# TensorE's expert program as a loop over pairs of experts instead of groups of four

## The reference, cut to what matters

```python
x = x + _L0_gnn_ref(_layernorm(x), adj, ...)         # attention with adj as bias, then a feed-forward net
x = x + _L0_ffn_ref(_layernorm(x), ...)
# in _L0_ffn_ref, with E1 = 8 outer and E2 = 4 inner experts, DIM = 384, HID = 1024:
slots2 = einsum('bGksd,bGksem->bGkemd', yn, disp2)    # 256 rows for each of the 32 experts (k, e)
u = einsum('bGkemd,kedh->bGkemh', slots2, w1) + b1
v, gate = split(u, 2, axis=-1)
act = v * gelu(gate)
o = einsum('bGkemh,kehd->bGkemd', act, w2) + b2
out2 = einsum('bGkpd,bGksp->bGksd', o, comb2)
out = einsum('bGPd,bGgP->bGgd', out2, comb1)
```

## Time and profile before

| | us |
|---|---|
| median of 3 runs | 3081.5 (3080.99 to 3088.55) |
| the profiled execution, own time | 3075.87 |
| its span, first to last instruction | 3074.1 |
| span of the experts' stage on TensorE, first expert matmul to last | 2141.69 to 2999.57 |
| mean granted TensorE clock | 0.975 of full speed |

### The profile page before, as it was taken

How to read it: one execution, slowest core, us unless ns; L and a number is a source line. 1 busy time by engine, 2 the same in 40 slices (tenths; PEclk the granted TensorE clock), 3 DMA queues, 4 the chain that set the end, 5 groups by cost and what they waited for, 6 DMA issues and landing times. The chain is left out here.

```text
span 3074.1 us, 63137 instructions
## 1 busy us (share of the span) xinstructions
PE 2860.1 (93%) x21971; PEld 2754.7 (90%) x21971; DVE 1899.1 (62%) x3029; ACT 1510.8 (49%) x3986; POOL 1474.9 (48%) x1486
## 2 busy tenths in 40 slices
PE   2899999999999999999999848997999999999996
PEld 2899999999999999999999738997999999999993
DVE  3466666666666666666666425664776766676764
ACT  3355554545454555545554425675454444454540
POOL 0344444343534444443444324552776766676760
PEclk9899999999999999999999969998999999999999
DMA  3010101010100101010101034553666656665899
GB/s 130 13 42 26 46 26 46 26 46 25 42 28 31 41 26 46 26 46 26 46 26 41 20 94 119 150 148 119 200 209 199 209 182 198 193 208 173 252 322 340
DMA packets 276793, 321.59 MB, mean 105 GB/s; under 512 B 17304, under 2 KB 275608, under 8 KB 276504
## 3 DMA queue, kind: packets, MB, share of 16 engines
q1 hardware_dynamic: 267960, 307.17, 32.1%
q10 hardware_dynamic: 8704, 12.58, 1.1%
HBM read 260.97 MB, written 58.72 MB: 104 GB/s over the span
## 5 line engine op out<-in xcount | busy, mean ns | idle before, releaser
L1567 PE MATMUL u_bank<-x_in,x_w 128*128 128x256 f32 x4608 | 584.1, 286 | 28.5 <-issue 20.8
L1567 PEld LDWEIGHTS u_bank<-x_in,x_w 128*128 128x128 f32 x4608 | 576.9, 194 | 31.4 <-issue 31.4
L949 POOL TENSOR_TENSOR hT_lo<-h_tmp,hT_hi 128x512 fp32r<-128x512 f32 x192 | 246.6, 1285 | 454.3 <-DVE hT_hi L838 453.1
L1724 POOL TENSOR_TENSOR x_aT<-x_act,x_aT 128x512 fp32r<-128x512 f32 x128 | 299.3, 2339 | 216.7 <-ACT x_aT L1632 216.7
L411 PE MATMUL m_bank<-yT_hi,w_hi 128*128 128x256 f32 x1152 | 341.5, 296 | 1.5 <-ACT h_tmp L683 1.5
L1623 ACT ACTIVATE x_gelu<-u_bank,x_b1T 128x256 f32<-128x256 f32 x256 | 121.4, 474 | 444.9 <-PE u_bank L1567 444.9
L411 PE MATMUL m_bank<-yT_hi,w_lo 128*128 128x256 f32 x1152 | 323.4, 281 | 0.0
L411 PE MATMUL m_bank<-yT_lo,w_hi 128*128 128x256 f32 x1152 | 323.4, 281 | 0.0
L1720 POOL TENSOR_TENSOR x_w<-expert_raw,x_w 128x768 fp32r<-128x768 f32 x128 | 274.3, 2143 | 102.1 <-DVE x_w L1663 102.1
L683 ACT ACTIVATE h_tmp<-m_bank,b1c 128x256 f32<-128x256 f32 x384 | 156.9, 470 | 273.5 <-PE m_bank L411 273.1
L1579 PE MATMUL o_bank<-x_w,x_aT 128*128 128x384 f32 x1536 | 289.3, 336 | 1.8 <-POOL x_aT L1724 1.8
(11 more groups left out here) (216 smaller groups left out, 6939.2 us busy)
## 6 DMA issues: line engine op xcount, KB each, us to landing
expert_raw<-in_L_ffn_w_dram SPq DMA_DIRECT2D x384, 384.0 KB, 5.0
ws_raw<-in_L_ffn_w_slot_dram SPq DMA_DIRECT2D x32, 576.0 KB, 7.1
x_in<-in_x_dram SPq DMA_DIRECT2D x32, 384.0 KB, 3.4
x_res<-in_x_dram SPq DMA_DIRECT2D x32, 384.0 KB
residual<-f_sb SPq DMA_DIRECT2D x32, 384.0 KB, 2.5
yn<-yn_sb SPq DMA_DIRECT2D x32, 384.0 KB, 2.5
expert_out<-x_o SPq DMA_DIRECT2D x64, 192.0 KB, 3.2
slots2T<-residual SPq DMA_DIRECT2D x8, 1536.0 KB, 11.7
```

Source lines behind the costliest of these rows:

```text
L949: nc.gpsimd.tensor_tensor(hT[i % 3][1][:], h_tmp[i % 2][:], hT[i % 3][0][:].bitcast(F32), ALU.subtract).then_inc(hl.sem, 1)
L1567: mm = pe.matmul(u_bank[n % BANKS][:, g, :], w1s[i % 2][a][:, c, g, c2 * P:(c2 + 1) * P], xT[e % 2][b][:, c, :], start=c == 0 and j == 0, ...
L1724: nc.gpsimd.tensor_tensor(aTs[i % 2][1][:], aT[i % 2][:], aTs[i % 2][0][:].bitcast(F32), ALU.subtract).then_inc(al.sem, 1)
```

## The change

TensorE no longer uses over_experts. Its program writes out two experts, then has a loop over pairs, from 1 to 14, with two experts in its body, and then two experts again. So there are 14 trips and 13 taken branches. body loses the argument k, which it did not use, and the parity e takes the place of e from 0 to 3; down(x - 1, 1 - e, ...) names the other parity's bank. The calls for each expert, their order, the buffers and the waited values are the same as before. The other four engines keep their loops over groups of four.

```diff
-            def body(x, k, e):
+            def body(x, e):
                 up(x, e, 0)
                 if past(x, 1):
-                    down(x - 1, (e - 1) % E2, PIECES - 1)
+                    down(x - 1, 1 - e, PIECES - 1)
                 for i in range(1, PIECES):
                     up(x, e, i)
                     down(x, e, i - 1)
-            over_experts(pe, body)
-            down(NX - 1, E2 - 1, PIECES - 1)
+            for e in range(2):
+                body(e, e)
+            with pe.Fori(1, NX // 2 - 1) as pair:
+                for e in range(2):
+                    body(pair * 2 + e, e)
+            for e in range(2):
+                body(NX - 2 + e, e)
+            down(NX - 1, 1, PIECES - 1)
```

## The result

The median is 3043.7 us (3041.47 to 3048.47, 4 runs) against 3081.24 us (3076.13 to 3088.55, 4 runs) before: a ratio of 0.9878, with a 95% interval of 0.9855 to 0.9902. The profiled execution took 3044.84 us, its span is 3043.1 us.

The account below looks back on a forecast made before the run. TensorE was taken to bound the kernel, losing 34.3 us at five back edges of its experts' loop; all other terms were 0. 3075.87 - 34.3 = 3041.6 us, or 3047.2 from the median; forecast 3045 us, range 3037 to 3057.

Parts of the forecast that it names:

- the loss of 34.3 us: Experts' stage, 125 units between down groups: 833.45 us against 799.1 without stalls, lost at five taken back edges of TensorE's loop.
- a lower clock: 11.4 us of the 34.3 us, at four of five back edges, taken for a consequence of TensorE's 22.9 us of gaps.
- Why an edge stalls: At each taken back edge the trip's whole program is read again through q8; two gaps wait for the first pieces.
- expected some 40: Sign of being right: instruction queue q8 brings some 40 transfers instead of 95.
- The trip gets shorter: TensorE's experts' loop: a pair's 768 matmuls and loads, below the layer's 859, stay on the engine; -34.3 us.
- what could make it wrong: Room on the engine depends on more than length, such as where the loop begins among the blocks q8 brings.
- More back edges: TensorE's pair loop has 13 taken branches: taken as 0 us, bounded from above by 13 x 0.46 = 6 us.
- The other engines' cover: DVE, POOL, ACT and DMA have 30% to spare in an undisturbed trip, so they do not hold TensorE up: 0 us.
- two cases for how the runs differ: Median falls to 3041.6 us if runs differ by stall length, to 3047.2 us if by something else.
- The pair doesn't stay either: Rival: the pair's program is read again at 13 edges, 6.86 us each, 89 us in all, 3134 us; chance 0.06.
- no change: Rival: DVE, POOL or weights' transfers fall behind over 32 experts and take up the time, up to 3081 us; chance 0.03.
- the clock drops stay: Rival: only the gaps go and lower clock remains there or elsewhere; gain 22.9 us, 3056 us; chance 0.04.

Follow-up runs that it names:

- experiment 7: The change with 56 more already-met wait instructions (112 waits) at the end of each pair trip on TensorE: 3127.51 us, ratio to before 1.0144.
- experiment 8: The change with 36 more already-met wait instructions (72 waits) at the end of each pair trip on TensorE: 3070.51 us, ratio to before 0.9961.
- experiment 2: The kernel before with 64 more instructions (already-met waits) on TensorE ahead of the first expert, loop over groups of four kept: 3046.2 us, ratio 0.9893.
- experiment 3: The kernel before with 256 more instructions (already-met waits) in TensorE's set-up, a whole block: 3081.66 us, ratio 1.0004.
- experiment 4: The kernel before with 200 more instructions (400 already-met waits) in TensorE's set-up, single run: 3046.72 us, against 3083.74 us for the kernel before.
- experiment 9: The change with 32 more instructions (64 already-met waits) in TensorE's set-up, single run: 3042.3 us.
- experiment 5: The kernel before with six experts in TensorE's loop body, four ahead and four behind, 3 taken edges: 3062.72 us, ratio 0.9934.
- experiment 1: The change with four experts in TensorE's loop body instead of two, head and tail of two kept, 6 taken edges: 3071.66 us, ratio to before 0.9966.

## Why the prediction was right

*What bounds the kernel, and the loss of 34.3 us.* The stretch of 125 units fell from 833.45 to 799.16 us, 34.3 us less, as the sum had it (833.45 - 799.1). Both parts went, the 22.9 us of gaps and the 11.4 us that the prediction calls a lower clock. That the clock's fall follows from the gaps was inferred from five edges; experiments 7 and 8 show it with idle time of another origin. The size of the clock's part was too large. At the first edge, where the clock stayed 1.00, the window is 3.60 us too long and the gaps are 3.06, so 0.54 is neither; at that rate 2.7 us of the 11.4 are the rest that experiment 8 shows without a lower clock, and some 8.7 us are clock. The sum of both, and so the forecast, is not touched by it.

*Why an edge stalls.* The reading was that the trip's program is fetched again. q8 with 41 blocks instead of 95 fits it (expected some 40), and every kernel with gaps has its 9 blocks for each missed edge of a group of four, or 12 for one of six. Nine is one more than the eight blocks of the trip.

*The trip gets shorter, and so stays.* The step was right, by a comparison with the layer's loop. Its ground was coarser than the cause. The text read the limit as a length, between the layer's trip (909 instructions; its 859 matmuls and loads are 856 by the trace's branches, the window took in a few more) and the group's 1,611. Experiments 2 to 4 show that 1,611 stay as well if they lie in 7 blocks, and not if they lie in 8. The prediction named this as what could make it wrong; it could not do so for a pair, whose 807 lie in 4 or 5 blocks (experiment 9). Seven stay, and eight do so only when no further block is brought, which fits a store of eight blocks of which one is the block read ahead, past the loop's end. That size is an estimate from these runs: five blocks (experiment 9) and seven (2 and 4) stay, eight are read again at every taken edge of the kernel before and of experiment 3, and eleven in experiment 5. That one block of the eight is taken by reading ahead is my reading of where the limit lies. Experiment 1 fits it: the branch comes some 24 instructions into the eighth block, and at the one edge that didn't miss q8 had brought nothing; in the kernel before the branch comes some 40 into it, and its five edges all miss. One such edge was traced, so this detail is argued, not shown.

*More back edges, 0 us.* Right: 799.16 us with 13 taken edges and with none. The upper bound of 6 us did not count.

*The other engines' cover.* Right: no new wait in the stage.

*The base.* 3043.7 lies between the prediction's two cases for how the runs differ, 3041.6 and 3047.2 us, and the kernels without gaps spread over about 7 us themselves (3041.47 to 3048.47), so that some of the spread has other causes. Outside of the 125 units the profiled execution after took 3.3 us longer than that of before, in parts that the change leaves alone: the stage began 1.8 us later, and what follows the last but one down group took 2.0 us longer, less 0.6 at the first matmuls.

*The rivals.* "The pair doesn't stay either" (0.06) is out by the q8 row, "no change" (0.03) by the waits, "the clock drops stay" (0.04) by the clock of 1.00 over the stage.

## What to carry to other kernels

If an engine idles with the releaser "issue" at the same place of every trip of a loop, look at the instruction queue over that trip: transfers in each trip mean that the loop's program is read again. On TensorE here, loops in four to seven blocks of about 256 instructions (every matmul counts two, with its weight load) ran their back edges for nothing; a loop in eight blocks cost 6.9 us per edge and one in eleven 6.3, gaps and lower clock together. Halving a trip that just doesn't fit cost nothing at either of the two places tried, and unrolling it entirely gained nothing over that.

## What was not expected of the hardware

Where a loop lies in the program can be worth 1.1% of a kernel without a change to the loop: 64 idle instructions ahead of it took 3079.89 to 3046.2 us. And one program at the limit (experiment 1) missed at five of its six edges in the execution traced, while its runs took from 3055.31 to 3079.55 us.
